# Idle transposes between TensorE's calls in the tail of a transformer block, with places and turned weights in another bank

## The chip, the cores and the metric

The kernel runs on 1 core of one Trainium2 chip. The metric is the device time in microseconds (us), the median over runs of the same program.

## The reference

One block of a Perceiver-like model in float32, over 32 sequences of 32 positions and 256 features (1024 rows, held as 8 tiles of 128 rows, four sequences in each):

```python
x = x + cross_attention(layernorm(x), ctx, ctx, mask)   # ctx: 32 x 257 x 256, 16 heads of 16
x = x + self_attention(layernorm(x))                    # causal, rotary, 16 heads
x = x + experts(layernorm(x))

# experts, in 8 groups of 128 rows, 8 experts, 32 places for each expert in each group:
raw = softmax(x @ router_w); idx1, idx2 = the two largest
p1 = cumsum(m1) - m1                      # place of a row in its expert's list
p2 = cumsum(m2) - m2 + count(m1)
combine = gate1 * onehot(idx1) * onehot(p1) + gate2 * onehot(idx2) * onehot(p2)   # where p < 32
dispatch = combine != 0
inp = einsum('GSEC,GSM->EGCM', dispatch, x)
hidden = gelu(inp @ w0) * (inp @ w1)      # 256 -> 1368
out = einsum('EGCM,GSEC->GSM', hidden @ wo, combine)
```

## The kernel before, in words

Five engines run programs of their own and meet at semaphores. The work has four stretches.

1. Preparation: weights are turned on TensorE and split in a rounded high part and a low part. A product of two such operands is three matmuls (`product3`, L213 to L217).
2. The attention pipeline (L750 to L790, to about 296 us): a loop over the 8 tiles, in which cross attention of a tile's four sequences overlaps with self attention of the tile before and the router of the one before that.
3. The tail (about 296 to 360 us): what remains of the last three tiles, `y_ - 1` = 5, `y_` = 6 and `z` = 7. Each engine has its calls in an order written out by hand: TensorE from L832, ScalarE from L1169, VectorE from L1639, GpSimd from L1855. Here cross attention's last projection is done (`project_cross`), self attention of tiles 6 and 7 (`project_self`, `turn_qk`, `scores`, `turn_self_probs`, `self_outputs`, `project_out`), the router of tiles 5 to 7 (`turn_router`, `logits`, `choose`), the places of rows (`positions` on TensorE, `place_early` and `slots_of` on VectorE), the weights of the combination (`weigh`, L1564 to L1567, 128x256 for each tile), and the dispatch (`disperse` L1619 on VectorE, `dispatch` L815 on TensorE, `keep_inputs` L1160 on ScalarE). `turn_weights_of` (L829) transposes the weights of two tiles, and `keep_weights_of` (L1166) copies them out.
4. The experts (360 to 553 us): 88 steps of 18 matmuls each, `up` and `down`, and then the combination (L925) and the store.

An engine works strictly in the order of its calls, so a wait holds everything written behind it. PSUM has eight banks, `bk[0]` to `bk[7]`. In the tail `bk[4]` belongs to tile 7, `bk[6]` to tile 6, `bk[7]` to tile 5, and the scores lie in the upper parts of banks 0 to 3. `positions(0, EARLY)` (tiles 0 to 4 in one call) writes to bank 5, the even dispatches to banks 5 and 2, the turned weights to bank 3. VectorE's `choose_early(1)` picks the second expert of tiles 0 to 4. The experts can begin when all of XT_hi and XT_lo is written (semaphore r_x_kept) and all four pairs of turned weights are copied out (ct_read).

Of the kernel before, what the change touches and what calls it, by code (L numbers as in the profile page):

```python
# [64 lines left out]
def program(nc, stack, x, ctx_in, mask, weights, xbq, xbk, xbv, xbo, router, w0, w1, wo, table, out):  # L65
# [205 lines left out]

    def positions_at(t):

        return bk[{0: 5, TT - 3: 7, TT - 2: 6, TT - 1: 4}[t]]

    def last_at(t):

# [1 line left out]

    def inputs_of(t):  # L280

        return (bk[0], bk[1]) if t % 2 else (bk[5], bk[2])

    crossed_T = bk[7][:, D:2 * D]

# [142 lines left out]
    def _(pe):  # L428
# [184 lines left out]
        def project_cross(t):  # L613
            if not exists(t, TT):
                return
            pe.wait_ge(sm["a_oT_hi"], t + 1)
            pe.wait_ge(sm["a_oT_lo"], t + 1)
            if isinstance(t, int) and t == TT - 1:
                pe.wait_ge(sm["pt1_ready"], B)
            for k in range(KH):  # L620
                last = product3(pe, front(t)[:, 0:D], OT_hi[:, k, :], OT_lo[:, k, :], WT_hi[:, 3, k, :], WT_lo[:, 3, k, :],
                                k == 0, k == KH - 1)
            last.then_inc(sm["a_wo_made"], 1)


        def turn_norm(t):
            if not exists(t, TT):
                return
            pe.wait_ge(sm["b_y"], t + 1)
            for k in range(KH):  # L630
                last = pe.transpose(front(t)[:, k * P:(k + 1) * P], y1[:, k * P:(k + 1) * P], ident)
            last.then_inc(sm["b_yT_made"], 1)

        def project_self(t, of_values):
            if not exists(t, TT):
                return
            if of_values:
                pe.wait_ge(sm["b_cos"], t + 1)
                pe.wait_ge(sm["b_sin"], t + 1)
            else:  # L640
                pe.wait_ge(sm["b_yT_hi"], t + 1)
                pe.wait_ge(sm["b_yT_lo"], t + 1)
            for n, i in enumerate((6,) if of_values else (4, 5)):
                for k in range(KH):
                    last = product3(pe, front(t)[:, n * D:n * D + D], yT_hi[:, k, :], yT_lo[:, k, :],
                                    WT_hi[:, i, k, :], WT_lo[:, i, k, :], k == 0, k == KH - 1)
            last.then_inc(sm["b_v_made" if of_values else "b_qk_made"], 1)
# [29 lines left out]
        def turn_self_probs(t):  # L677

            if not exists(t, TT):
                return  # L680
            pe.wait_ge(sm["b_pn"], t + 1)
            pe.wait_ge(sm["b_scaled"], t + 1)
            for g in range(G):
                last = pe.transpose(spare(t)[:, g, :], pr2[:, g, :, :], ident)  # L684
            last.then_inc(sm["b_pT_made"], 1)

        def after_self(t, scored):

            if not exists(t, TT):
                return  # L690
            if scored:
                pe.wait_ge(sm["b_scaled"], t + 1)
            else:
                pe.wait_ge(sm["b_pT_act"], t + 1)
                pe.wait_ge(sm["b_pT_dve"], t + 1)
# [20 lines left out]
        def project_out(t):  # L716
            if not exists(t, TT):
                return
            pe.wait_ge(sm["b_oT_hi"], t + 1)
            pe.wait_ge(sm["b_oT_lo"], t + 1)  # L720
            if isinstance(t, int) and t == TT - 3:
                pe.wait_ge(sm["a_sum"], TT)
            for k in range(KH):
                last = product3(pe, back(t)[:, 0:D], O2T_hi[:, k, :], O2T_lo[:, k, :], WT_hi[:, 7, k, :], WT_lo[:, 7, k, :],
                                k == 0, k == KH - 1)
            last.then_inc(sm["b_wo_made"], 1)
# [67 lines left out]
        def positions(t0, t1):  # L794

            n = (t1 - t0) * E
            pe.wait_ge(sm["r_chosen"], max(t0 - EARLY + 2, 1))
            if t0 == 0:
                pe.wait_ge(sm["a_lT"], TT)
            at_ = positions_at(t0)  # L800
            pe.matmul(at_[:, 0:2 * n], before, chosen[:, :, t0:t1, :], start=True, stop=True)
            pe.matmul(at_[:, 2 * n:3 * n], ones[:, :], chosen[:, 0, t0:t1, :], start=True, stop=True)              .then_inc(sm["r_pos_made"], 1)

        def dispatch(t):
# [11 lines left out]
                                     start=True, stop=True)  # L816
            last.then_inc(sm["r_x_made"], 1)

        def turn_weights_of(i):

            pe.wait_ge(sm["r_weighed"], 2 * i + 2)
            if i >= 1:
                pe.wait_ge(sm["ct_read"], i)
            else:
                pe.wait_ge(sm["b_pT_act"], TT)
                pe.wait_ge(sm["b_pT_dve"], TT)
            for q in range(4):
                t, k = 2 * i + q // 2, q % 2
                last = pe.transpose(bk[3][:, q * P:(q + 1) * P], C_all[:, t, k * P:(k + 1) * P], ident)  # L829
            last.then_inc(sm["ct_made"], 1)  # L830

        y_, z = TT - 2, TT - 1  # L832
        project_self(y_, True)
        after_self(y_ - 1, False)
        turn_probs(B - 1, (B - 1) % 4, 0)
        turn_probs(B - 1, (B - 1) % 4, 1)
        turn_qk(y_)
# [2 lines left out]
        turn_last(z)  # L840
        scores(y_)
        project_cross(z)
        project_out(y_ - 1)
        turn_norm(z)
        project_self(z, False)
        turn_self_probs(y_)
        project_self(z, True)
        turn_qk(z)
        self_outputs(y_)
        scores(z)  # L850
        turn_router(y_ - 1)
        logits(y_ - 1)
        turn_self_probs(z)
        project_out(y_)
        self_outputs(z)
        positions(0, EARLY)
        project_out(z)
        turn_router(y_)
        turn_router(z)
        logits(y_)  # L860
        dispatch(0)
        positions(y_ - 1, y_)
        dispatch(1)
        logits(z)
        dispatch(2)
        positions(y_, z)
        dispatch(3)
        dispatch(4)
        turn_weights_of(0)
        turn_weights_of(1)  # L870
        turn_weights_of(2)
        positions(z, TT)
        dispatch(y_ - 1)
        dispatch(y_)
        dispatch(z)
        turn_weights_of(3)
        pe.wait_ge(sm["r_x_kept"], TT)
        pe.wait_ge(sm["ct_read"], 4)

# [50 lines left out]
    def _(ac):  # L930
# [114 lines left out]
        def split_norm(t):  # L1045
            keep(t, "b_yT_made", yT_hi[:, :, :], halves(front(t)[:, 0:D]), "b_yT_hi")

        def keep_self_keys(t):
            keep(t, "b_qkT_made", kT[:, :, :], halves(front(t)[:, D:2 * D]), "b_kT")
# [113 lines left out]

        def keep_weights_of(i):
            ac.wait_ge(sm["ct_made"], i + 1)
            ac.activation(CT[:, 2 * i:2 * i + 2, :, :], bk[3].rearrange("p (t k n) -> p t k n", t=2, k=2), ACT.Copy)\  # L1166
              .then_inc(sm["ct_read"], 1)

        y_, z = TT - 2, TT - 1  # L1169
        keep_self_values(y_)  # L1170
        keep_probs(B - 1, (B - 1) % 4)
        keep_self_keys(y_)
        keep_last(z)
        split_cross(z)
        self_exp(y_)
        split_norm(z)
        spread_probs(y_)
        keep_self_values(z)
        keep_self_keys(z)
        self_exp(z)  # L1180
        split_self(y_)
        keep_router(y_ - 1)
        spread_probs(z)
        split_self(z)
        keep_router(y_)
        router_exp(y_ - 1)
        router_exp(y_)
        keep_router(z)
        keep_inputs(0)
        router_exp(z)  # L1190
        keep_inputs(1)
        keep_inputs(2)
        keep_inputs(3)
        keep_weights_of(0)
        keep_weights_of(1)
        keep_inputs(4)
        keep_weights_of(2)
        keep_inputs(y_ - 1)
        for n in range(3):
            split(0, n)  # L1200
        keep_inputs(y_)
        keep_inputs(z)
        keep_weights_of(3)
# [18 lines left out]
    def _(ve):  # L1222
# [425 lines left out]
        add_and_norm(z, "b", 0)  # L1648
        shift_scores(y_)
        add_and_norm(z, "b", 1)  # L1650
        split_norm(z)
        add_probs(y_)
        choose_early(1)
        scale_probs(y_)
        rotate(z)
        add_rotated(z)
        spread_probs(y_)
        add_and_norm(y_ - 1, "c", 0)
        spread_queries(z)
        scale_scores(z)  # L1660
        shift_scores(z)
        add_and_norm(y_ - 1, "c", 1)
        add_probs(z)
        scale_probs(z)
        split_self(y_)
        spread_probs(z)
        read_logits(y_ - 1)
        add_and_norm(y_, "c", 0)
        split_self(z)
        place_early()  # L1670
        weigh(0)
        add_and_norm(y_, "c", 1)
        add_and_norm(z, "c", 0)
        disperse(0)
        choose(y_ - 1)
        add_and_norm(z, "c", 1)
        weigh(1)
        weigh(2)
        disperse(1)
        weigh(3)  # L1680
        weigh(4)
        read_logits(y_)
        disperse(2)
        choose(y_)
        read_logits(z)
        disperse(3)
        slots_of(y_ - 1)
        disperse(4)
        choose(z)
        weigh(y_ - 1)  # L1690
        slots_of(y_)
        disperse(y_ - 1)
        weigh(y_)
        slots_of(z)
        disperse(y_)
        weigh(z)
# [210 lines left out]
```

## Time and profile before

| what | us |
|---|---|
| median of 3 runs | 563.48 |
| lowest, highest | 556.87, 567.03 |
| the profiled execution's own time | 566.69 |
| its span | 564.8 |
| TensorE busy, share of the span | 501.6 (89%) |
| VectorE busy | 406.2 (72%) |
| ScalarE busy | 325.1 (58%) |
| GpSimd busy | 247.3 (44%) |

The span runs from the first to the last instruction; 1.9 us of the profiled execution lie around it. The granted clock is the share of full speed that TensorE's throttle let through; its mean over this span is 0.940.

### The profile page before, as it was taken

To read this page: it belongs to the slowest core of one execution; us is meant where nothing else is said; L and a number is where in the kernel's file an instruction comes from. 1 tells how busy PE (TensorE), PEld (TensorE's weight loads), DVE (VectorE), ACT (ScalarE), POOL (GpSimd) and SP (SyncE) were. 2 spreads that over 40 slices of the span, in tenths; PEclk is the share of its full clock that TensorE was granted. 3 is DMA by queue.
4 is the path that set the end of the run, shared out by engine and by line. 5 is a ranking of instruction groups with operands and counts; after the bars stand their busy time and mean duration, and the time that the engine had idled before them with its cause. 6 is when DMAs were issued, how large, how long until landed. Compare 5 with 4: busy or idle time off the path is not lost.

```text
span 564.8 us, 18262 instructions
## 1 busy us (share of the span) xinstructions
PE 501.6 (89%) x6637; PEld 460.1 (81%) x6637; DVE 406.2 (72%) x1005; ACT 325.1 (58%) x839; POOL 247.3 (44%) x337
## 2 busy tenths in 40 slices
PE   0777999989999999999976657899999999999996
PEld 0656778878889898888865546799999999999995
DVE  6414346477666767676676788599999999999973
ACT  0325667577667757676752215666665766657650
POOL 1301153344445364444430120366667667676650
PEclk9989899999999999999996765599999999999998
DMA  7420111121111111120006200055655656465302
GB/s 217 129 94 19 38 43 40 27 55 22 42 39 35 26 33 38 21 54 2 4 2 200 102 0 1 5 196 167 188 158 189 198 174 195 146 187 188 113 1 74
DMA packets 57981, 48.91 MB, mean 87 GB/s; under 512 B 20926, under 2 KB 49600, under 8 KB 57920
## 3 DMA queue, kind: packets, MB, share of 16 engines
q1 hardware_dynamic: 57920, 48.09, 28.9%
q8 instruction: 39, 0.64, 0.5%
q14 instruction: 22, 0.18, 0.1%
HBM read 46.86 MB, written 1.08 MB: 85 GB/s over the span
## 4 chain that ended last, share of the span: by engine, by line
PE 77%; ACT 7%; DVE 5%; issue 5%; DMA 2%; SPq 2%; POOL 0%; DVEq 0%; ACTq 0%; POOLq 0%
PE bank L215 20%; PE bank L217 18%; PE bank L216 18%; PE bank L556 5%; PE bank L534 3%; PE bank L580 3%; ACT Pr L994 2%; PE bank L491 2%; PE bank L925 2%; PE bank L711 1%; ACT PTd L1087 1%; DMA bias_raw<-in_L_xattn_bv 1%; PE bank L673 1%; DMA last_prob<-Pr 1%; PE bank L684 1%
## 5 line engine op out<-in xcount | busy, mean ns | idle before, releaser
L215 PE MATMUL bank<-XT_lo,W_hi 128*128 128x256 f32 (+1 forms) x352 | 100.5, 286 | 1.3 <-ACT CT L1166 1.3
L216 PE MATMUL bank<-XT_hi,W_lo 128*128 128x256 f32 (+1 forms) x352 | 100.1, 284 | 0.0
L217 PE MATMUL bank<-XT_hi,W_hi 128*128 128x256 f32 (+1 forms) x352 | 99.8, 284 | 0.0
L1876 POOL TENSOR_TENSOR W_lo<-raw,W_hi 128x256 fp32r<-128x256 f32 (+1 forms) x88 | 88.4, 1005 | 7.0
L1799 POOL TENSOR_TENSOR Pr<-Pr,rinv 128x1028 f32<-128x1028 f32 x31 | 58.9, 1901 | 51.1 <-DVE rinv L1307 50.4
L994 ACT ACTIVATE Pr<-Sc,nmax 128x257 f32<-128x257 f32 x128 | 63.8, 502 | 23.1 <-DVE nmax L1296 21.6
L1296 DVE CUSTOM_DVE_ANT_0 Sc<-bank,mask_add 128x257 f32<-128x257 f32 x128 | 46.9, 422 | 38.8 <-PE bank L534 16.8
L1738 DVE TENSOR_TENSOR hid_lo<-hid,hid_hi 128x256 fp32r<-128x256 f32 (+1 forms) x88 | 73.1, 831 | 1.5 <-ACT hid_hi L1215 1.5
L1708 DVE TENSOR_TENSOR W_lo<-raw,W_hi 128x512 fp32r<-128x512 f32 (+1 forms) x88 | 68.8, 784 | 5.2 <-ACT W_hi L1139 1.4
L1874 POOL CAST W_hi<-raw 128x256 fp32r<-128x256 f32 (+1 forms) x88 | 39.1, 444 | 74.3 <-PE bank L217 36.9
L215 PEld LDWEIGHTS bank<-XT_lo,W_hi 128*128 128x128 f32 (+1 forms) x352 | 66.6, 189 | 1.6 <-issue 1.6
L216 PEld LDWEIGHTS bank<-XT_hi,W_lo 128*128 128x128 f32 (+1 forms) x352 | 66.4, 189 | 0.0
L217 PEld LDWEIGHTS bank<-XT_hi,W_hi 128*128 128x128 f32 (+1 forms) x352 | 66.3, 188 | 0.0
L1211 ACT ACTIVATE act<-bank 128x256 f32<-128x256 f32 (+1 forms) x88 | 33.7, 383 | 53.9 <-PE bank L217 53.3
L1139 ACT ACTIVATE W_hi<-raw 128x512 fp32r<-128x512 f32 (+1 forms) x88 | 53.6, 612 | 0.0
L215 PE MATMUL bank<-W_lo,hid_hi 128*128 128x256 f32 (+1 forms) x176 | 49.7, 282 | 0.5 <-issue 0.5
L216 PE MATMUL bank<-W_hi,hid_lo 128*128 128x256 f32 (+1 forms) x176 | 49.5, 281 | 0.0
L217 PE MATMUL bank<-W_hi,hid_hi 128*128 128x256 f32 (+1 forms) x176 | 49.5, 281 | 0.0
L1215 ACT ACTIVATE hid_hi<-hid 128x256 fp32r<-128x256 f32 (+1 forms) x88 | 36.9, 419 | 14.2 <-DVE hid L1733 12.3
L1733 DVE TENSOR_TENSOR hid<-bank,act 128x256 f32<-128x256 f32 (+1 forms) x88 | 36.4, 414 | 11.8 <-ACT act L1211 11.5
L215 PE MATMUL bank<-WT_lo,ctxT_hi 128*128 128x256 f32 x128 | 40.1, 314 | 4.7 <-ACT KT L971 4.5
L215 PE MATMUL bank<-ctxT_lo,WT_hi 128*128 128x256 f32 x128 | 39.4, 308 | 1.5 <-DVE ctxT_lo L1281 1.5
(234 smaller groups left out, 1333.4 us busy)
## 6 DMA issues: line engine op xcount, KB each, us to landing
raw<-in_L_ffn_w_kernel SPq DMA_DIRECT2D x32, 512.0 KB, 4.6
ctx_raw<-in_ctx SPq DMA_DIRECT2D x32, 256.0 KB, 2.8
raw<-in_L_ffn_wo_kernel SPq DMA_DIRECT2D x16, 512.0 KB, 5.8
raw<-in_L_ffn_w_kernel SPq DMA_DIRECT2D x16, 344.0 KB
last_prob<-Pr SPq DMA_DIRECT2D x128, 1.0 KB, 1.8
raw<-in_L_ffn_wo_kernel SPq DMA_DIRECT2D x8, 256.0 KB
x_sb<-in_x SPq DMA_DIRECT2D x4, 256.0 KB, 3.9
VL_all<-vl_rows SPq DMA_DIRECT2D x8, 128.0 KB
```

The lines of the kernel that those rows point to most:

```text
L215: pe.matmul(dst, a_hi, b_lo, start=first, stop=False)
L216: pe.matmul(dst, a_lo, b_hi, start=False, stop=False)
L217: return pe.matmul(dst, a_hi, b_hi, start=False, stop=last)
L994: ac.activation(Pr[:, r % 2, g, 0:SC], Sc[:, r % 2, g, 0:SC], ACT.Exp, bias=nmax[:, r % 2, g:g + 1], scale=-1.0, accum_out=Pr[:, r % 2, g, ...
L1139: ac.activation(W01_hi[:, (NT * half_ + n) % RW, :, :, 0:w].rearrange("p i k n -> p (i k) n"), raw01[:, :, :, t * P:t * P + w].rearrange(" ...
L1215: ac.activation(hid_hi[0:w, m % RW, :], hid[0:w, m % RH, :], ACT.Copy).then_inc(sm["hhi_done"], 1)
L1296: ve.tensor_tensor_reduce(Sc[:, r % 2, g, 0:SC], bk[g][:, 0:SC], mask_add[:, :], -0.25, 3e38, ALU.add, ALU.min, nmax[:, r % 2, g:g + 1]).t ...
L1708: ve.tensor_tensor(W01_lo[:, (NT * half_ + n) % RW, :, :, 0:w].rearrange("p i k n -> p (i k) n"), raw01[:, :, :, t * P:t * P + w].rearrang ...
L1738: ve.tensor_tensor(hid_lo[0:w, m % RW, :], hid[0:w, m % RH, :], f(hid_hi[0:w, m % RW, :]), ALU.subtract)\
L1799: po.tensor_tensor(Pr[:, r % 2, :, 0:SC], Pr[:, r % 2, :, 0:SC], rinv[:, r % 2, :].unsqueeze(2).broadcast_to([P, G, SC]), ALU.mult).then_i ...
L1874: po.tensor_copy(W2_hi[0:w, m % RW, :], raw2[0:w, t, :]).then_inc(sm["hi2"], 1)
L1876: po.tensor_tensor(W2_lo[0:w, m % RW, :], raw2[0:w, t, :], f(W2_hi[0:w, m % RW, :]), ALU.subtract)\
```

## The change

The tail alone changes.

- A new function `keep_busy(4)` issues four transposes of the identity into bank 5. They wait for nothing and nobody reads them. 34 such groups (136 transposes) stand between TensorE's calls, from behind `project_cross(z)` to behind `turn_weights_of(3)`.
- So that bank 5 is free, `positions(0, EARLY)` writes to bank 7, the even dispatches to banks 2 and 3, and the turned weights to bank 7. Waits come with it: `positions(0, EARLY)` waits for the read logits of tile 5, `positions` of tile 5 for the first weighing, `turn_weights_of(0)` for the fifth r_slot, which is an instruction of VectorE's `weigh(y_ - 1)`.
- Calls change places. TensorE: `after_self` ahead of `project_self(y_, True)`. ScalarE: `keep_probs` ahead of `keep_self_values(y_)`, `keep_self_values(z)` ahead of `spread_probs(y_)`, `split_self(y_)` ahead of `self_exp(z)`, `router_exp(y_ - 1)` ahead of `split_self(z)`, `keep_inputs(y_ - 1)` behind the first three splits of the expert weights, and others. VectorE: `choose_early(1)` ahead of `split_norm(z)`, `spread_probs(y_)` ahead of `add_rotated(z)`, `split_self(y_)` ahead of `scale_probs(z)`, `add_and_norm(y_, "c", 1)` ahead of `weigh(0)`, `choose(y_ - 1)` ahead of `disperse(0)`, `slots_of(y_ - 1)` and `weigh(4)` ahead of `read_logits(z)`, `weigh(y_ - 1)` ahead of `choose(z)`.

```diff
-        return bk[{0: 5, TT - 3: 7, TT - 2: 6, TT - 1: 4}[t]]
+        return bk[{0: 7, TT - 3: 7, TT - 2: 6, TT - 1: 4}[t]]
...
-        return (bk[0], bk[1]) if t % 2 else (bk[5], bk[2])
+        return (bk[0], bk[1]) if t % 2 else (bk[2], bk[3])
...
             if t0 == 0:
-                pe.wait_ge(sm["a_lT"], TT)
+                pe.wait_ge(sm["r_neg"], 1)
+            elif t0 == EARLY:
+                pe.wait_ge(sm["r_weighed"], 1)
...
+        def keep_busy(n):
+
+            for _ in range(n):
+                pe.transpose(bk[5][:, 0:P], ident, ident)
+
         def turn_weights_of(i):
...
             else:
-                pe.wait_ge(sm["b_pT_act"], TT)
-                pe.wait_ge(sm["b_pT_dve"], TT)
+                pe.wait_ge(sm["r_slot"], PLACE)
...
-                last = pe.transpose(bk[3][:, q * P:(q + 1) * P], C_all[:, t, k * P:(k + 1) * P], ident)
+                last = pe.transpose(bk[7][:, q * P:(q + 1) * P], C_all[:, t, k * P:(k + 1) * P], ident)
```

TensorE's calls after the change, from `project_cross(z)` on, with [n] for n groups of four idle transposes:

```
project_cross(z) [1] project_out(y_ - 1) [1] turn_norm(z) [1] project_self(z, False) [1]
turn_self_probs(y_) [1] project_self(z, True) [3] turn_qk(z) self_outputs(y_) scores(z) [1]
turn_router(y_ - 1) logits(y_ - 1) [1] turn_self_probs(z) project_out(y_) [2] self_outputs(z)
positions(0, EARLY) [1] project_out(z) [1] turn_router(y_) [3] turn_router(z) [1] logits(y_)
dispatch(0) [1] positions(y_ - 1, y_) [2] dispatch(1) [2] logits(z) [1] dispatch(2) [1]
positions(y_, z) dispatch(3) [2] dispatch(4) turn_weights_of(0) [1] turn_weights_of(1) [1]
turn_weights_of(2) positions(z, TT) dispatch(y_ - 1) [3] dispatch(y_) dispatch(z) [1]
turn_weights_of(3) [1]
```

## Rows read from the trace of the kernel before

**Rows 1.** Stretches of the span: busy us and instructions per engine, granted clock, DMA.
```profile
core 0: us, PE busy (x) PEld busy (x) DVE busy (x) ACT busy (x) POOL busy (x), PEclk, DMA share, GB/s
366.00:546.00 180.00, 180.00 (x1519) 180.00 (x1518) 168.95 (x268) 117.33 (x268) 121.57 (x168) 1.00 0.53 165
...
310.00:314.00 4.00, 3.75 (x16) 3.38 (x16) 3.22 (x10) 0.03 (x1) 0.00 (x0) 0.50 1.07 377
...
335.00:344.00 9.00, 5.14 (x22) 4.78 (x22) 8.40 (x31) 1.61 (x5) 1.71 (x3) 0.50 0.00 1
344.00:350.00 6.00, 4.99 (x21) 4.41 (x21) 5.06 (x30) 3.94 (x10) 0.00 (x0) 0.50 0.00 0
```

**Rows 2.** Timeline, TensorE: first matmuls of the experts, slow and then fast.
```profile
360.27 0.55 PE L215 MATMUL bank<-XT_lo,W_hi 128*128 128x256 f32 x1 [1.25 <-ACT CT L1166]
...
365.53 0.36 PE L215 MATMUL bank<-XT_lo,W_hi 128*128 128x256 f32 x1
```

**Rows 3.** Timeline, TensorE: transposes and small matmuls of the tail at both paces.
```profile
308.42 0.69 PE L631 MATMUL bank<-tab,y 128*128 128x128 f32 x2 [2.00 <-DVE y L1347]
...
316.13 0.64 PE L655 MATMUL bank<-tab,qk 128*128 128x128 f32 x4 [0.62 <-ACT Vm L1017]
...
343.10 1.02 PE L742 MATMUL bank<-router_sb,yTf 128*128 128x8 f32 x4 [1.88 <-ACT yTf L1017]
...
350.24 1.09 PE L829 MATMUL bank<-tab,C_all 128*128 128x128 f32 x4 [0.78 <-ACT CT L1166]
```

**Rows 4.** Chain of waits, in order of time, from the dispatches on.
```profile
346.44 2.17 PE bank L815 x8
348.61 0.87 PE bank L829 x4
...
359.38 0.65 ACT CT L1166
```

**Rows 5.** Timeline of the preparation: 16 transposes, and the next wide matmuls.
```profile
23.92 3.62 PE L446 MATMUL bank<-tab,xn 128*128 128x128 f32 x16
29.04 0.47 PE L215 MATMUL bank<-xnT_lo,WT_hi 128*128 128x512 f32 x1 [1.50 <-DVE xnT_lo L1245]
29.36 0.39 PE L216 MATMUL bank<-xnT_hi,WT_lo 128*128 128x512 f32 x1
```

**Rows 6.** Stretches: transposes and 32-column matmuls alone, then the clock.
```profile
297.00:299.00 2.00, 2.00 (x12) 1.85 (x12) 0.56 (x1) 0.60 (x1) 0.00 (x0) 0.61 0.07 1
299.00:301.00 2.00, 2.00 (x130) 1.79 (x128) 1.65 (x9) 0.39 (x1) 0.45 (x1) 0.54 0.08 5
301.00:303.00 2.00, 1.11 (x70) 0.82 (x59) 1.66 (x5) 0.75 (x3) 0.18 (x1) 1.00 0.38 48
...
314.00:316.00 2.00, 0.94 (x6) 0.77 (x6) 1.92 (x5) 1.53 (x3) 0.00 (x0) 0.88 0.25 77
```

**Rows 7.** Timeline: second choice of tiles 0 to 4, and tile 7's values.
```profile
310.78 0.14 DVE L1487 TENSOR_REDUCE gate<-rest 128x5 f32<-128x40 f32 x1
...
311.65 0.20 DVE L1494 TENSOR_TENSOR chosen<-tab,lowest 128x40 f32<-128x40 f32 x1
...
315.61 0.38 ACT L1017 ACTIVATE Vm<-bank 128x256 f32<-128x256 f32 x1 [0.45 <-PE bank L217]
```

**Rows 8.** Timeline around the turned weights and VectorE's weighing of tile 5.
```profile
348.41 1.05 PE L829 MATMUL bank<-tab,C_all 128*128 128x128 f32 x4
...
348.97 0.40 DVE L1565 TENSOR_SCALAR C_all<-tab,slot_of,gate 128x256 f32<-128x256 f32 x1
```

**Rows 9.** Waits of 310 to 360 us: who waited for what, total, times, longest.
```profile
PE bank L734 <- DVE y L1347: 8.1, 3, 3.8
...
ACT CT L1166 <- PE bank L829: 2.3, 3, 1.3
...
DVE pos L1545 <- PE bank L802: 1.5, 1, 1.5
```

More of the change, by code:

```diff
@@ L824, in turn_weights_of @@
             else:
-                pe.wait_ge(sm["b_pT_act"], TT)
-                pe.wait_ge(sm["b_pT_dve"], TT)
+                pe.wait_ge(sm["r_slot"], PLACE)
             for q in range(4):
                 t, k = 2 * i + q // 2, q % 2
-                last = pe.transpose(bk[3][:, q * P:(q + 1) * P], C_all[:, t, k * P:(k + 1) * P], ident)
+                last = pe.transpose(bk[7][:, q * P:(q + 1) * P], C_all[:, t, k * P:(k + 1) * P], ident)
             last.then_inc(sm["ct_made"], 1)
         y_, z = TT - 2, TT - 1
+        after_self(y_ - 1, False)
         project_self(y_, True)
-        after_self(y_ - 1, False)
         turn_probs(B - 1, (B - 1) % 4, 0)
@@ L842, in _ @@
         project_cross(z)
+        keep_busy(4)
         project_out(y_ - 1)
+        keep_busy(4)
         turn_norm(z)
+        keep_busy(4)
         project_self(z, False)
+        keep_busy(4)
         turn_self_probs(y_)
+        keep_busy(4)
         project_self(z, True)
+        keep_busy(4)
+        keep_busy(4)
+        keep_busy(4)
         turn_qk(z)
@@ L850, in _ @@
         scores(z)
+        keep_busy(4)
         turn_router(y_ - 1)
         logits(y_ - 1)
+        keep_busy(4)
         turn_self_probs(z)
         project_out(y_)
+        keep_busy(4)
+        keep_busy(4)
         self_outputs(z)
         positions(0, EARLY)
+        keep_busy(4)
         project_out(z)
+        keep_busy(4)
         turn_router(y_)
+        keep_busy(4)
+        keep_busy(4)
+        keep_busy(4)
         turn_router(z)
+        keep_busy(4)
         logits(y_)
         dispatch(0)
+        keep_busy(4)
         positions(y_ - 1, y_)
+        keep_busy(4)
+        keep_busy(4)
         dispatch(1)
+        keep_busy(4)
+        keep_busy(4)
         logits(z)
+        keep_busy(4)
         dispatch(2)
+        keep_busy(4)
         positions(y_, z)
         dispatch(3)
+        keep_busy(4)
+        keep_busy(4)
         dispatch(4)
         turn_weights_of(0)
+        keep_busy(4)
         turn_weights_of(1)
+        keep_busy(4)
         turn_weights_of(2)
@@ L873, in _ @@
         dispatch(y_ - 1)
+        keep_busy(4)
+        keep_busy(4)
+        keep_busy(4)
         dispatch(y_)
         dispatch(z)
+        keep_busy(4)
         turn_weights_of(3)
+        keep_busy(4)
         pe.wait_ge(sm["r_x_kept"], TT)
@@ L1165, in keep_weights_of @@
             ac.wait_ge(sm["ct_made"], i + 1)
-            ac.activation(CT[:, 2 * i:2 * i + 2, :, :], bk[3].rearrange("p (t k n) -> p t k n", t=2, k=2), ACT.Copy)\
+            ac.activation(CT[:, 2 * i:2 * i + 2, :, :], bk[7].rearrange("p (t k n) -> p t k n", t=2, k=2), ACT.Copy)\
               .then_inc(sm["ct_read"], 1)
         y_, z = TT - 2, TT - 1
+        keep_probs(B - 1, (B - 1) % 4)
         keep_self_values(y_)
-        keep_probs(B - 1, (B - 1) % 4)
         keep_self_keys(y_)
@@ L1176, in _ @@
         split_norm(z)
+        keep_self_values(z)
         spread_probs(y_)
-        keep_self_values(z)
         keep_self_keys(z)
+        split_self(y_)
         self_exp(z)
-        split_self(y_)
         keep_router(y_ - 1)
         spread_probs(z)
+        router_exp(y_ - 1)
         split_self(z)
         keep_router(y_)
-        router_exp(y_ - 1)
+        keep_router(z)
         router_exp(y_)
-        keep_router(z)
         keep_inputs(0)
+        keep_inputs(1)
         router_exp(z)
-        keep_inputs(1)
         keep_inputs(2)
@@ L1197, in _ @@
         keep_weights_of(2)
-        keep_inputs(y_ - 1)
         for n in range(3):
             split(0, n)
+        keep_inputs(y_ - 1)
         keep_inputs(y_)
@@ L1650, in _ @@
         add_and_norm(z, "b", 1)
+        choose_early(1)
         split_norm(z)
         add_probs(y_)
-        choose_early(1)
         scale_probs(y_)
         rotate(z)
+        spread_probs(y_)
         add_rotated(z)
-        spread_probs(y_)
         add_and_norm(y_ - 1, "c", 0)
@@ L1663, in _ @@
         add_probs(z)
+        split_self(y_)
         scale_probs(z)
-        split_self(y_)
         spread_probs(z)
@@ L1670, in _ @@
         place_early()
+        add_and_norm(y_, "c", 1)
         weigh(0)
-        add_and_norm(y_, "c", 1)
         add_and_norm(z, "c", 0)
+        choose(y_ - 1)
         disperse(0)
-        choose(y_ - 1)
         add_and_norm(z, "c", 1)
@@ L1680, in _ @@
         weigh(3)
-        weigh(4)
         read_logits(y_)
@@ L1684, in _ @@
         choose(y_)
+        slots_of(y_ - 1)
+        weigh(4)
         read_logits(z)
         disperse(3)
-        slots_of(y_ - 1)
         disperse(4)
+        weigh(y_ - 1)
         choose(z)
-        weigh(y_ - 1)
         slots_of(y_)
+        weigh(y_)
         disperse(y_ - 1)
-        weigh(y_)
         slots_of(z)
```

## The prediction

> **What bounds the kernel now.** I read the share of each engine in stretches of the span first. From 366 to 546 us TensorE is busy all of the time at full clock [rows 1]; those 1519 matmuls at 118 ns set the time of the experts, and nothing that the change touches makes them fewer. Next the tail, 296 to 360 us. There VectorE is the fullest engine: 8.40 of 9 us between 335 and 344 us, where TensorE has 5.14 [rows 1]. The granted clock of TensorE is 0.50, its 1.2 GHz level, from 331 us on until the experts are well under way; in all of 335 to 350 us the row says 0.50. So two things hold the tail: VectorE's own work, and in places TensorE's calls at half pace. The chain of waits shows where the second is so: 2.17 us for two dispatches and 0.87 us for a group of turned weights [rows 4]. The list of waits says the same from the other side: of TensorE's waits the longest are for VectorE (`turn_router` for y, 8.1 us in three waits), and what others wait for TensorE is short (2.3 and 1.5 us) [rows 9].
>
> **What half pace costs.** A 128x256 matmul starts every 118 ns at full clock (180 us by 1519, rows 1). From 360.27 to 365.53 us 25 of them start, one each 210 ns [rows 2]. At full clock the same 25 take 2.96 us instead of 5.26: 2.3 us, wholly on the path, because behind them TensorE doesn't pause until the end of the experts. The tail's own pieces: four transposes last 0.64 us at full clock and 1.09 at half, so with a last one of 0.27 and 0.42 us a group of four takes TensorE's time for about 0.48 and 0.87 us [rows 3, 4]; two transposes 0.69 against about 0.39; the four of `logits` 1.02 against about 0.6 (estimate, in the same ratio) [rows 3]; two dispatches 2.17 against about 1.0 for eight matmuls at 118 ns [rows 4].
>
> **The idle transposes.** 34 groups take 34 x 0.48 = 16.3 us of TensorE at full clock and 34 x 0.87 = 29.6 at half. They read and write nothing that another engine uses; only TensorE's order makes a call behind them late. To see what of it is on the path I walked the calls of the four engines in their orders, from 294 us to the experts' first matmul: a call starts when its engine is free and what it waits for is there, and lasts as its row does. The old order, at the clock that the records show, ends at 357.9 us in this walk where the trace has 360.27 [rows 2], so I use differences only.
> - Old order, full clock all through: 353.8, that is 4.1 us earlier than the old order at the shown clock. No more, though the half-paced calls on the chain hold some 6.5 us, since VectorE's 49 us of work take over: in that walk it never pauses from 328 us to the end.
> - New order with the groups, full clock all through: 353.5 (4.3 us earlier). Without the groups it is 353.3: the groups fill pauses, TensorE has 42.8 us of work in 59.
> - New order with the groups, half clock all through: 372.1, 14.2 us later. TensorE would have 73 us of work and bound the tail.
>
> **Which clock it will be.** Neither end. The trace shows rises behind stretches in which TensorE hardly paused: 310 to 314 us has 3.75 of 4 us busy at 0.50, and 314 to 316 us a mean of 0.88 [rows 1, 6]; 344 to 350 us has 4.99 of 6, with gaps, and no rise [rows 1]; the experts' start has no gap and rises after 5.3 us [rows 2]. Falls stand behind sparse stretches, such as 1.11 of 2 us from 301 to 303 us [rows 6]. At half clock the groups leave TensorE with hardly a gap, so it climbs; at full clock it is busy about 42.8 of 59 us, which is near the stretches that fell where the work is thinnest (`scores(z)` to `turn_router(y_ - 1)`, where even with a group some 2 us stay empty while VectorE shifts scores, and `turn_router(z)`, 3.4 us). So I take one or two falls, each with some us of half pace, in which the groups stand in the way: three of them ahead of `turn_qk(z)` cost 2.6 us at half pace, of which 2 are late. Walks of the new order with one to three such stretches end between 355.1 and 359.6 us, mostly 356 to 358.5; I take 356.5, 1.4 us earlier than 357.9.
>
> **Do idle transposes count as work?** The matmuls of 512 columns behind 16 transposes start 230 ns apart at 29.36 us, a pace of full clock, while the transposes took 226 ns each, half pace (the clock row reads 1.00 there all the time; the durations decide) [rows 5]. Between them TensorE had nothing. And 297 to 301 us hold only 12 transposes and 130 small instructions at a clock of 0.61 and 0.54; then it reads 1.00 [rows 6]. So transposes did go ahead of rises.
> The Trainium skill (TensorE: Matmul & The Clock Gate, Part 4: PE-mode transpose) says that a transpose doesn't count as TensorE's activity the way other matmuls do. By that the groups would be dead time; the two rises above speak against it.
>
> **The rest of the change.**
> - `positions(0, EARLY)` in bank 7 waits for logits read at 327.0 us, before it ran at 328.6: nothing. The weighing that the next `positions` waits for is 7 us old there: nothing.
> - `turn_weights_of(0)` now waits for VectorE's second step of weighing tile 5. Before, it ran at 348.41 and that step at 348.97 to 349.37 [rows 8]: 1 us late if the order stayed. But `weigh(y_ - 1)` moves ahead of `choose(z)` (2.1 us), so the wait is met before dispatch 4 ends. Nothing; 1 us if that cover goes, with `turn_weights_of(1)`, (2) and two dispatches queued behind it.
> - `choose_early(1)`, 310.78 to 311.85 us, five small dependent steps [rows 7], moves into VectorE's pause while tile 7's norm is transposed (308.4 to 309.5): 1.07 us off VectorE, but what follows waits for TensorE's projection until 313.0. Gain nothing at half clock, up to 0.5 at full.
> - `spread_probs(y_)` (1.4 us) ahead of `add_rotated(z)` makes b_rope 1.3 us later, just beside tile 7's values, 315.61 + 0.38 = 315.99 [rows 7]: 0 to 0.4 us late. On ScalarE `spread_probs(y_)` stands behind those values: 0 to 0.8 us late, with `self_outputs(y_)` behind. The last splits of the expert weights ahead of `keep_inputs(y_ - 1)` are off the last part of ScalarE's queue, 1.6 us between two dispatch copies; in the walk that is the most of the 0.3 us that the new order is worth.
> All of these are within the walks.
>
> **The sum.** 566.69 of the profiled execution, less 1.4 in the tail, less 2.3 at the experts' start (TensorE is dense in the last 10 us before it, so full clock is there): 563.0. That execution lies 3.2 above the median of 563.48, and its tail was nearly the worst that the clock can do to it (0.50 for the last 34 us). Part of the 3.2 is thus what the change takes away; I leave the new median 2.5 below 563.0: 560.5.
>
> **The rivals.**
> 1. Full clock throughout: 566.69 - 4.3 - 2.3 = 560.1, less the same 2.5: 557.6. For it: 72% mean use with the gaps spread. Against: two pauses over 2 us that no group can fill. Chance 0.25.
> 2. The groups only pay for themselves: the falls come where three groups stand, the walk ends at 359.6 (+1.7), the experts gain 2.3: 566.1, and 564 to 566 as a median. For it: 0.87 us a group at half pace. Chance 0.18.
> 3. Slower: transposes don't raise the clock, TensorE is the bound of the tail at half pace and still slow at the experts: 566.69 + 14.2 = 580.9, 578 as a median. It decides as soon as a group in a dense stretch of the tail leaves the clock at 0.50 for more than 10 us. Against it: rows 5 and 6. Chance 0.05. By the page's rule above this is the outcome.
> 4. The attention pipeline ahead of the tail and the end are untouched; nothing there moves. That the walk misses 2.4 us of the old tail leaves room for a larger gain, 5 or more beyond rival 1, below 552: chance 0.05.
> My forecast, 559 to 563: 0.47.
>
> **Range.** 553.5 to 567: from rival 1 less 4 (three runs of before spread over 10 us) to rival 2 with 1 us. A change of under 2% (11 us) is no more than runs of this kernel differ. Faster by over 2% needs 552.2 or less: 0.06; slower by over 2%: 0.05; within: 0.89.
>
> **What the profile after would show.** Right: a clock near 1.00 in most of 335 to 350 us and at the first expert matmul, these 118 ns apart; the experts' first matmul at 355 to 359 us; transposes into bank 5 lasting 0.27 us; VectorE without pauses from 330 us. Wrong: a clock of 0.50 over dense idle transposes (rival 3); `turn_weights_of(0)` waiting for VectorE; or a first matmul before 353 us, which would mean that VectorE was not the floor.

## The result and the profile after

The changed kernel takes 558.38 us (median of 12 runs, 554.31 to 561.23), the kernel before 564.77 us in 12 runs beside it (556.87 to 567.36). The ratio run against run is 0.9926, 95% interval 0.9901 to 0.9952: faster, by 0.5 to 1.0%. Twelve more runs of the changed kernel (e8), with 23 of the kernel before beside them, give 558.58 against 563.67 us, ratio 0.9897 (0.9862 to 0.9932). The profiled execution takes 558.36 us, its span is 556.4 us, 8.4 less than before.

The page of the changed kernel, engines in 40 slices of the span; the tail is in slices 22 to 26, and its clock there reads 9, 8, 8, 7, 9:

```profile
span 556.4 us, 18537 instructions
...
PE   0777999899999999999975779999999999999996
...
PEclk9999999989999999999999887999999999999998
```

Its stretches, with the columns of [rows 1]:

```profile
303.00:304.00 1.00, 0.00 (x0) 0.00 (x0) 0.97 (x2) 0.00 (x0) 0.54 (x1) 1.00 1.08 374
...
306.00:310.00 4.00, 3.94 (x21) 3.96 (x22) 2.45 (x6) 0.00 (x0) 0.00 (x0) 0.58 1.08 379
...
316.00:321.00 5.00, 2.56 (x16) 1.94 (x15) 3.91 (x8) 1.01 (x2) 1.12 (x2) 0.86 0.00 0
321.00:324.00 3.00, 3.00 (x25) 2.83 (x27) 2.13 (x6) 1.57 (x4) 0.00 (x0) 0.67 0.00 0
...
331.00:335.00 4.00, 2.14 (x12) 2.14 (x13) 3.79 (x12) 0.18 (x1) 1.87 (x4) 0.78 0.00 0
335.00:344.00 9.00, 9.00 (x62) 9.00 (x62) 7.88 (x39) 4.48 (x12) 0.00 (x0) 0.72 0.00 1
344.00:350.00 6.00, 5.32 (x46) 4.88 (x45) 4.87 (x30) 4.49 (x10) 0.00 (x0) 1.00 0.01 3
...
355.00:360.00 5.00, 5.00 (x44) 5.00 (x44) 3.52 (x6) 3.67 (x9) 4.76 (x8) 1.00 0.00 0
```

Against [rows 1]: 335 to 344 us reads 0.72 where it read 0.50, 344 to 350 us reads 1.00. The clock falls three times, each time behind a stretch in which TensorE is nearly empty and VectorE nearly full (303 to 304, 316 to 318, 329 to 333 us), and it is back at 1.00 after 3.4, 3.4 and 6.8 us of mostly dense work. The experts have 44 matmuls in the five us from 355, full pace. The timeline at their start, against [rows 2]:

```profile
354.26 0.36 PE L215 MATMUL bank<-XT_lo,W_hi 128*128 128x256 f32 x1 [0.56 <-ACT CT L1206]
```

And the idle transposes (line 824), all of them:

```profile
L824 PE MATMUL bank<-tab x136: 270/273/456, 301.2 to 353.4; 128*128 128x128 f32 x136
```

The three figures in ns are the shortest, the median and the longest: half of them last 0.27 us or less, as those of [rows 3] at full clock. No instruction waits for their result, but they stand in front of TensorE's own next call, as shown below.

To see where time went I divided each profile at two marks: the start of GpSimd's last cross-attention step (`Ot<-VL_all,last_prob`; the code before it is the same in all kernels), and the experts' first matmul. All in us, from the profiles:

| kernel | first mark | tail, first mark to first expert matmul | first expert matmul to end of span | median, ratio to before |
|---|---|---|---|---|
| before | 300.55 | 59.72 | 204.53 | 564.77 |
| changed | 297.06 | 57.20 | 202.14 | 558.38, 0.9926 |
| changed, again (e8) | 299.97 | 56.25 | 202.18 | 558.58, 0.9897 |
| e1 no groups | 301.12 | 59.92 | 204.66 | 563.58, 0.9990 |
| e2 old order, groups | 297.58 | 59.24 | 202.18 | 560.31, 0.9920 |
| e3 late groups | 296.26 | 59.50 | 202.14 | 559.64, 0.9899 |
| e12 late groups, again | 296.11 | 59.50 | 202.09 | 560.06, 0.9911 |
| e9 early groups | 295.47 | 58.00 | 201.93 | 558.41, 0.9880 |
| e4 matmuls for transposes | 295.80 | 58.01 | 202.19 | 558.80, 0.9885 |
| e6 gaps filled | 296.31 | 55.47 | 201.92 | 556.50, 0.9878 |
| e11 old order, gaps filled | 298.53 | 58.95 | 201.92 | 557.78, 0.9869 |
| e10 all filled | 295.06 | 54.17 | 200.97 | 553.06, 0.9790 |

So of the 8.4 us between the two profiles 3.5 lie ahead of the tail, in code that the change doesn't touch; the same program (changed, e8) has 2.9 us between its own two profiles there. 2.5 us (3.5 in e8) are the tail's and 2.4 the experts'. That is 4.9 to 5.9 us of the change's own, beside 6.4 and 5.1 between medians.

Within the tail the gain lies late. From the first turned weights to the experts' first matmul (the kernel before, then the changed one):

```profile
348.41:360.27 11.86, 8.18 (x33) 6.53 (x33) 8.02 (x32) 8.43 (x17) 0.04 (x1) 0.50 0.01 1
```

```profile
344.80:354.26 9.46, 7.55 (x62) 6.73 (x61) 7.58 (x33) 7.98 (x16) 0.05 (x1) 1.00 0.01 2
```

Of the tail's 2.5 us 2.4 lie here, where the clock went from 0.50 to 1.00; the 47.9 us ahead of it became 47.7 (46.8 in e8).

What lies ahead of the tail has its own clock. These are the stretches at the start of the attention pipeline in the kernel before and in e12, whose first marks are 300.55 and 296.11 us:

```profile
38.00:62.00 24.00, 19.03 (x140) 16.92 (x139) 6.88 (x23) 11.62 (x32) 2.92 (x5) 0.79 0.15 40
```

```profile
38.00:62.00 24.00, 18.31 (x233) 15.54 (x234) 10.00 (x35) 13.63 (x39) 4.71 (x6) 1.00 0.15 44
```

In the profiles of the table the clock of this stretch and the first mark go together: 0.96 to 1.00 with first marks of 295.06 to 297.06 us (changed, e3, e4, e6, e9, e10, e12), 0.79 to 0.86 with 297.58 to 301.12 us (before, e8, e1, e2, e11). The two profiles of the changed kernel, with the same code, read 1.00 and 0.86. Whole runs say the same: of the 15 of the kernel before beside e9 to e12, the five with a mean clock of 0.948 or more took 561.2 to 563.5 us, the ten with less 564.5 to 569.7. What makes the clock fall there in one execution and not in another stays open.

### The profile page after: what moved, and what is told of

Read it like the earlier page. It is cut to its first block, busy times and chain, and to the rows that moved or that the text cites. A ratio compares the mean times of both kernels' runs of the same rounds, so it can differ in the third digit from the quotient of the medians.

```text
span 556.4 us, 18537 instructions
## 1 busy us (share of the span) xinstructions
PE 502.3 (90%) x6773; PEld 463.1 (83%) x6773; DVE 404.8 (73%) x1005; ACT 324.9 (58%) x839; POOL 250.5 (45%) x337
## 4 chain that ended last, share of the span: by engine, by line
PE 78%; ACT 7%; issue 5%; DVE 4%; DMA 2%; SPq 2%; POOL 0%; DVEq 0%; ACTq 0%; POOLq 0%
PE bank L215 20%; PE bank L216 18%; PE bank L217 18%; PE bank L556 5%; PE bank L534 3%; PE bank L580 3%; ACT Pr L1034 2%; PE bank L491 2%; PE bank L824 2%; PE bank L965 2%; PE bank L711 1%; DMA bias_raw<-in_L_xattn_bv 1%; PE bank L673 1%; DMA last_prob<-Pr 1%; ACT PTd L1127 1%
## 5 line engine op out<-in xcount | busy, mean ns | idle before, releaser
L215 PE MATMUL bank<-XT_lo,W_hi 128*128 128x256 f32 (+1 forms) x352 | 99.3, 282 | 0.6 <-ACT CT L1206 0.6
L1916 POOL TENSOR_TENSOR W_lo<-raw,W_hi 128x256 fp32r<-128x256 f32 (+1 forms) x88 | 90.6, 1030 | 7.0
L1778 DVE TENSOR_TENSOR hid_lo<-hid,hid_hi 128x256 fp32r<-128x256 f32 (+1 forms) x88 | 74.9, 851 | 1.5 <-ACT hid_hi L1255 1.5
L1748 DVE TENSOR_TENSOR W_lo<-raw,W_hi 128x512 fp32r<-128x512 f32 (+1 forms) x88 | 66.5, 758 | 4.8 <-ACT W_hi L1179 1.1
L215 PEld LDWEIGHTS bank<-XT_lo,W_hi 128*128 128x128 f32 (+1 forms) x352 | 65.4, 186 | 0.8 <-issue 0.8
L216 PEld LDWEIGHTS bank<-XT_hi,W_lo 128*128 128x128 f32 (+1 forms) x352 | 65.2, 185 | 0.0
L1355 DVE COPY PT<-bank 128x512 f32<-128x512 f32 x32 | 22.1, 691 | 25.5 <-PE bank L556 25.3
```

Source lines behind the costliest of these rows:

```text
L215: pe.matmul(dst, a_hi, b_lo, start=first, stop=False)
L216: pe.matmul(dst, a_lo, b_hi, start=False, stop=False)
L1748: ve.tensor_tensor(W01_lo[:, (NT * half_ + n) % RW, :, :, 0:w].rearrange("p i k n -> p (i k) n"), raw01[:, :, :, t * P:t * P + w].rearrang ...
L1778: ve.tensor_tensor(hid_lo[0:w, m % RW, :], hid[0:w, m % RH, :], f(hid_hi[0:w, m % RW, :]), ALU.subtract)\
L1916: po.tensor_tensor(W2_lo[0:w, m % RW, :], raw2[0:w, t, :], f(W2_hi[0:w, m % RW, :]), ALU.subtract)\
```

## The experiments

**Is it the groups or the order?** e1 takes all 34 groups out, the rest as changed; this line each time:

```diff
-        keep_busy(4)
```

> The changed kernel without its 34 groups; banks, waits and orders as changed. My theory (the groups buy the clock and the clock buys the time): nearly all of the gain goes. The clock reads about 0.50 over most of the tail and at the experts' first matmuls, which start 0.21 us apart, and the ratio to the kernel before is 0.997 to 1.005. Rival (the new order of calls is the gain): the ratio stays at 0.992 to 0.994 at that same low clock.

Measured: 563.58 against 564.33 us, ratio 0.9990 (0.9962 to 1.0018). The tail is 59.92 us, the stretches of e1 read:

```profile
301.12:331.00 29.88, 19.92 (x255) 16.21 (x255) 21.16 (x52) 7.22 (x17) 3.40 (x6) 0.60 0.43 142
331.00:361.04 30.04, 18.46 (x78) 15.91 (x79) 24.21 (x105) 13.74 (x30) 2.82 (x6) 0.58 0.00 1
361.04:366.00 4.96, 4.96 (x23) 4.96 (x24) 1.51 (x3) 2.35 (x4) 4.64 (x8) 0.50 0.00 0
```

Half clock in most of the tail and at the experts' start, and no gain, as expected. At this clock the new order, with the new banks and waits, is worth nothing that shows.

**The old order with the groups.** e2 has the old sequences of all three engines, with the new banks and waits and the groups.

```diff
+        project_self(y_, True)
         after_self(y_ - 1, False)
-        project_self(y_, True)
...
-        choose_early(1)
         split_norm(z)
         add_probs(y_)
+        choose_early(1)
...
```

> Old order of calls on TensorE, ScalarE and VectorE, with the new banks and the 34 groups in their places between TensorE's calls. My theory: 0.990 to 0.995, about the whole gain, since the walks of both orders at full clock end 0.3 us apart. Rival (the order is the gain): 0.998 or more, though the clock is high.

Measured: 560.31 against 564.33 us, ratio 0.9920 (0.9882 to 0.9959), as I expected by the ratio. But the tail of its profile is 59.24 us, 2 to 3 longer than the changed kernel's, though its clock in the tail is as high (0.88 from mark to mark, as in the changed kernel). That is against the walks, which gave the order 0.3 us, though the half-paced stretches don't stand at the same calls in the two. e11 takes it up.

**Which groups?** e3 keeps the 9 behind `dispatch(4)`, e9 the 25 ahead of it.

Each takes out the same line as e1: e3 its 25 places from `project_cross(z)` to `dispatch(4)`, e9 its 9 places behind that.

> The changed kernel with only the 9 groups that stand behind dispatch(4); the 25 ahead of it are taken out. My theory: the tail up to dispatch(4) goes at half clock as before, then the clock rises at some point in the last 8 us ahead of the experts or not at all; if it rises, the experts' 2.3 us come back and the ratio is 0.995 to 0.998, if not it is 1.000. Rival (only the experts' start matters): 0.992, the full gain.

> The changed kernel with only the 25 groups ahead of dispatch(4) and none of the 9 behind. With e3 it splits the gain by place. My theory (each stretch of half clock taken away pays for itself where it stands): the tail up to dispatch(4) is as short as with the change; behind it the clock may fall again, then the experts' first matmuls start 0.21 us apart and 2.3 us are lost. Ratio 0.992 to 0.996. Rival (the end of the tail and the experts' start are all that counts, as the 4.7 us of e3 suggest): 0.997 or more.

e3: 559.64 against 564.33 us, 0.9899 (0.9867 to 0.9930). e9: 558.41 against 565.87 us, 0.9880 (0.9823 to 0.9937). Both ratios lie below what was expected (0.995 to 0.998 and 0.992 to 0.996). Stretches of e3, then of e9:

```profile
331.00:348.00 17.00, 11.48 (x50) 10.72 (x51) 15.27 (x73) 5.76 (x14) 2.77 (x5) 0.50 0.00 0
348.00:355.76 7.76, 6.14 (x50) 5.53 (x49) 5.52 (x20) 7.36 (x15) 0.04 (x1) 0.99 0.01 2
355.76:360.76 5.00, 5.00 (x42) 5.00 (x43) 2.78 (x5) 3.68 (x8) 4.68 (x8) 1.00 0.00 0
```

```profile
344.00:353.47 9.47, 4.74 (x35) 3.74 (x33) 7.60 (x33) 7.97 (x16) 0.05 (x1) 1.00 0.00 0
353.47:358.47 5.00, 5.00 (x29) 5.00 (x30) 1.62 (x3) 2.70 (x6) 4.68 (x8) 0.66 0.01 3
```

The profiles are as the theory has them. e3 keeps half clock until 348 us; then the clock comes up with the nine groups and the experts start at full pace, 42 matmuls in 5 us. Its tail is as long as the old one (59.50 against 59.72 us), but not in its parts: from the first turned weights on it takes 10.32 us where the kernel before takes 11.86, and ahead of them, at half clock nearly all the way, it is 1.3 us longer. e9 shortens the tail by 1.7 us, but the 9.47 us without late groups are half empty, the clock falls, and the experts start with 29 matmuls in 5 us: their last matmul comes 190.14 us after the first, against 188.66 in the changed kernel and 191.04 before. So the two sets work where they stand. In e9's profile the 1.5 us lost there come back at the very end, and the table's 201.93 us hides them: the clock happened to stay at 1.00 in the combination, whose 32 matmuls take 7.17 us instead of the 8.86 of the changed kernel. The medians don't show what the late groups add to the early ones: 558.41 us for e9, 558.38 and 558.58 for all 34. Nor are the medians what the profiles add up to: e3's marks explain 2.6 us, its median 4.7. So I ran it again (e12).

> The kernel of e3 once more, on another chip, since its 4.7 us were 2 us more than its profile explains (tail as long as before, experts 2.4 us shorter). If that was spread between runs: ratio 0.993 to 0.997. If it holds: 0.988 to 0.992 again, and something ahead of the tail or in it gains that one profile didn't show.

Measured: 560.06 against 565.87 us, 0.9911 (0.9881 to 0.9941). It holds, and its profile again has the old tail (59.50), 2.4 us less in the experts, and a first mark at 296.11 us, 4.4 earlier than before's. So it wasn't spread between a few runs, and what the two profiles gain beyond the experts lies ahead of the tail, where the code is the same and their clock is at 1.00 (above). Whether the late groups have a part in that is not shown: two profiles can't say whether it is more than the luck that moved the changed kernel's mark from 297.06 to 299.97.

**Do transposes count as activity?** e5 puts 100 of them in a row between the tail's last wait and the experts, in the kernel before, where the clock is 0.50.

```diff
         pe.wait_ge(sm["r_x_kept"], TT)
         pe.wait_ge(sm["ct_read"], 4)
+        for _ in range(100):
+            pe.transpose(bk[5][:, 0:P], ident, ident)
```

> The kernel before, with 100 idle transposes in one row between the last wait of the tail and the experts' first matmul, where its clock is 0.50. If transposes raise the clock: the first 16 to 32 start 0.21 us apart, the rest 0.12, the row lasts about 14 us, and the experts begin at full clock. If they don't: all 100 start 0.21 us apart, 21 us, the experts begin slow and their clock rises some 5 us in.

The row lasts 13.04 us and the kernel takes 573.26 us (one run). Timeline and stretches of e5:

```profile
358.13 13.04 PE L880 MATMUL bank<-tab 128*128 128x128 f32 x100 [1.14 <-ACT CT L1168]
370.92 0.36 PE L215 MATMUL bank<-XT_lo,W_hi 128*128 128x256 f32 x1
```

```profile
358.13:362.00 3.87, 3.87 (x19) 3.87 (x20) 0.00 (x0) 1.15 (x1) 0.00 (x0) 0.50 0.00 0
362.00:370.90 8.90, 8.90 (x83) 8.90 (x83) 0.00 (x0) 0.00 (x0) 1.47 (x4) 0.99 0.01 2
```

TensorE ran nothing but transposes in these 13 us: 0.20 us each for 3.9 us at 0.50 (1.2 GHz), then 0.107 us each at full clock (2.4 GHz). They count. The Trainium skill (TensorE: Matmul & The Clock Gate, Part 4: PE-mode transpose) has it that the full clock doesn't engage for transposes, beside figures for bf16; for these float32 transposes the measurement decides against it.

e4 asks the same in place: each idle transpose becomes an idle matmul with twice the columns.

```diff
-                pe.transpose(bk[5][:, 0:P], ident, ident)
+                pe.matmul(bk[5][:, 0:D], WT_hi[:, 3, 0, 0:P], WT_hi[:, 3, 0, :], start=True, stop=True)
```

> Each idle transpose is replaced by an idle matmul of 128x256 in float32r into the same bank: nearly the same time of TensorE (118 against 120 ns at full clock, 210 at half for both), but twice the columns. If transposes count as activity like matmuls, the time and the clock are the same as with the change (ratio 0.990 to 0.995, mean clock of the tail within 0.04 of 0.88). If they count for less, the clock falls less often and the ratio is lower by 0.002 or more.

558.80 against 564.33 us, 0.9885 (0.9845 to 0.9924); tail 58.01 us, its clock 0.88 as in the changed kernel. The ratio is 0.004 and 0.001 below those of the changed kernel (0.9926 and 0.9897); the intervals overlap, so the 0.002 of the expectation can't be told by it, and the clock of the tail shows no difference.

**What do the three falls cost?** e6 puts more into the empty stretches.

```diff
         project_out(y_ - 1)
-        keep_busy(4)
+        keep_busy(12)
         turn_norm(z)
-        keep_busy(4)
+        keep_busy(8)
...
         scores(z)
-        keep_busy(4)
+        keep_busy(18)
...
         turn_router(y_)
-        keep_busy(4)
-        keep_busy(4)
-        keep_busy(4)
+        keep_busy(36)
```

> The changed kernel with 44 more idle transposes in its three empty stretches: 8 more ahead of turn_norm(z), 4 more behind it, 14 more ahead of turn_router(y_ - 1), 24 instead of 12 more ahead of turn_router(z) in all 36. If the three falls of the clock (at 305.9, 319.2 and 333.3 us of the profile after) come from those stretches, the clock stays at 1.00 there and the tail is 1.5 to 3 us shorter than with the change: ratio 0.986 to 0.990. Rival (VectorE's work is the floor and the half-paced calls are hidden behind it): the clock stays up and the ratio is that of the change, 0.991 to 0.994.

The edit adds 8 + 4 + 14 + 24 = 50 idle transposes; the 44 of the expectation is a slip. Measured: 556.50 against 563.67 us, 0.9878 (0.9837 to 0.9919), beside 0.9897 of the changed kernel on the same chip (e8). The intervals overlap, so the medians don't settle it; the profile is clearer. From its first mark to 325 us its clock reads 1.00 throughout, one fall is left (340 to 344 us, 0.57), and the tail is 55.47 us, 0.8 and 1.7 less than the two profiles of the changed kernel.

```profile
296.31:325.00 28.69, 24.42 (x424) 21.18 (x414) 23.19 (x63) 7.23 (x17) 3.42 (x6) 1.00 0.45 149
325.00:351.78 26.78, 22.06 (x175) 20.65 (x174) 22.44 (x97) 13.41 (x30) 2.83 (x6) 0.94 0.00 1
340.00:344.00 4.00, 4.00 (x23) 3.70 (x22) 3.35 (x21) 1.92 (x4) 0.00 (x0) 0.57 0.01 4
```

> The changed kernel again, on the chip of the three runs beside it: 0.990 to 0.995.

Measured: 558.58 against 563.67 us, 0.9897 (0.9862 to 0.9932).

**Is TensorE's time free?** e7 doubles every group (`keep_busy(8)`).

> Each of the 34 groups has eight transposes instead of four, 16 us more of TensorE's time at full clock. TensorE's work in the tail is then 59 of 59 us, so it bounds the tail though its clock is 1.00 all through: 5 to 9 us longer than with the change, ratio 1.002 to 1.009. If it were no longer, TensorE's time in the tail would be free.

562.83 us, 4.3 above the changed kernel beside it and a little less than the 5 to 9 expected; ratio to before 0.9969 (0.9936 to 1.0002). Its mean clock is as high as e6's (both a median of 0.988 over their runs, 0.977 in the changed kernel), and nearly the whole gain is gone. So 16 us more of idle work on TensorE cost 4.3 us: the room for it is limited. Where the time is lost no profile shows.

**What is the order worth at full clock?** e11 is e2 with the larger groups of e6.

> The old orders of calls on all engines with the groups of e6, so that the clock is at full speed in nearly all of the tail: what is the order worth then? By the walks of the prediction 0.3 us: tail from Ot to the experts' first matmul 55.5 to 56.5 us against 55.5 of e6, ratio 0.986 to 0.989. Rival (the new order pays once TensorE is fast, as e2 hints): tail of 57 to 58.5 us, ratio 0.990 to 0.994.

557.78 against 565.87 us, 0.9869 (0.9825 to 0.9914), and a tail of 58.95 us against e6's 55.47. By the tail the rival holds, by the ratio the theory does: it is no higher than e6's 0.9878, and the medians lie 1.3 us apart in two batches of runs. The profile has to be read with care, for its execution is the slowest of e11's six (561.31 us) with the lowest mean clock (0.979, the others 0.988 to 0.994). Most of the 3.5 us goes with its clock:

```profile
298.53:308.61 10.08, 8.39 (x167) 7.93 (x159) 6.33 (x17) 1.68 (x4) 1.22 (x2) 0.66 0.80 256
```

From the first mark to `turn_norm(z)` it is 10.08 us here, at a mean clock of 0.66, and 7.74 in e6 at 1.00. That is 2.3 of the 3.5 us. That the old order brings this fall on is not shown; e2, with the same order, takes 7.54 us to `turn_norm(z)`. Half of the 2.3 us is a price of idle work when the clock has fallen all the same: the 12 transposes ahead of `turn_norm(z)` ran at half clock, and the norm waited behind them. TensorE and VectorE in e11's timeline:

```profile
306.10 2.68 PE L824 MATMUL bank<-tab 128*128 128x128 f32 x12
...
306.98 0.41 DVE L1385 TENSOR_SCALAR y<-x_sb,ln_mvb,ln_rb 128x256 f32<-128x256 f32 x1
...
308.61 0.38 PE L631 MATMUL bank<-tab,y 128*128 128x128 f32 x2
```

y is there at 307.39 and is turned at 308.61: 1.2 us late. From `turn_norm(z)` to the experts it is 48.87 us in e11 and 47.73 in e6, with a clock of 0.97 and 0.96. This 1.1 us is what the profiles leave for the order at a high clock. 0.5 of it lies between `turn_norm(z)` and `turn_router(y_ - 1)` (12.87 and 12.37 us), where `choose_early(1)` stands: in e11 it runs from 310.67 to 311.75, between the sums and `scale_probs`, and TensorE waits 0.3 us for the result; in e6 it runs in the pause before yT_lo, from 303.91 to 305.03.

**The best version.** e10 is e6 with the other idle places of the kernel filled too: 36 transposes into bank 6 while the attention pipeline fills, 20 ahead of the combination.

```diff
         turn_ctx(0, 0, 16)
+        fill(12)
         keys(0, 0)
+        fill(6)
         values(0, 0)
...
                 energies(b, u)
+                if early_ and u == 0:
+                    fill(7)
...
                     keys(b + 1, (u + 1) % 4)
+                    if early_:
+                        fill(11)
...
+        keep_busy(20)
         pe.wait_ge(sm["y_read_dve"], E + 1)
```

> The kernel of e6, with 36 more idle transposes in the gaps at the start of the attention pipeline (12 behind the first turn_ctx, 6 behind keys(0), 7 behind energies(0), 11 behind keys(1)) and 20 ahead of the combination at the very end. Theory (half clock costs wherever TensorE is on the path): the fall at about 40 us and the one ahead of the combination go, 1 to 3 us and 1 us less than e6, ratio 0.980 to 0.986, and the best version so far. Rival (there the other engines hold the pace, or the row only delays the first real calls): as e6, 0.986 to 0.990.

553.06 against 565.87 us, ratio 0.9790 (0.9748 to 0.9832), and a spread of only 3.1 us over 6 runs. Its stretches:

```profile
295.06:325.00 29.94, 25.70 (x433) 22.56 (x424) 24.54 (x65) 7.62 (x18) 3.40 (x6) 1.00 0.43 143
325.00:349.23 24.23, 19.15 (x161) 17.78 (x160) 21.07 (x94) 13.14 (x29) 2.87 (x6) 1.00 0.00 1
...
537.00:550.20 13.20, 10.05 (x58) 8.90 (x58) 4.72 (x11) 1.17 (x2) 0.00 (x0) 1.00 0.24 81
```

1.00 in all of the tail, which takes 54.17 us, and at the end, where the combination's 32 matmuls take 7.07 us instead of 8.61 in e6, and the end of the span comes 0.95 us sooner. e9's 7.17 us without any filler there show that the clock sometimes stays up by itself, so one profile each doesn't prove what the 20 transposes are worth. Nor does the first mark: 295.06 us here, 295.47 to 296.26 in the three profiles of e9, e3 and e12, whose clock was at 1.00 from 38 to 62 us without fillers. All six runs lie below every run of the changed kernel and of the kernel before (554.01 at most, 554.31 at least). More transposes later in the pipeline were not tried.

## Why the prediction held, and where it was off

- The mechanism was right: the groups buy the clock (e1 without them 0.9990), the clock gives TensorE's calls back, and the rule that spoke against it (rival 3) fell to e5.
- The term for the experts' start, 2.3 us, measured 2.4: the last expert matmul comes 191.04 us after the first before, 188.66 after.
- The term for the tail, 1.4 us, was too small: 2.5 and 3.5 us in two profiles. I had "one or two falls"; there are three, at about the places named, with 3.4, 3.4 and 6.8 us of half pace (e8 has a fourth around its first mark, 15 us in all). So the falls were not fewer than assumed; what they cost was. 2.4 us of the gain lie behind the first turned weights, where no fall stood.
- The walks gave the order 0.3 us. At half clock none of it shows (e1). At high clock it is 1.1 us between e11 and e6 from `turn_norm(z)` on, and 2 to 3 us between the tails of e2 and of the changed kernel, whose falls stand elsewhere; the medians don't tell it from nothing. So 0.3 looks too small, and by how much stays open. "Up to 0.5 at full" for `choose_early(1)` agrees with the 0.5 us of its stretch.
- VectorE as the floor of the tail is right in kind and was put too high: in e10, at 1.00 throughout, VectorE is busy 21.07 of the last 24.23 us, but the walk gave 4.3 us as the most that the clock can return, and e10's tail has 5.55 less than before.
- "Three of them ahead of `turn_qk(z)` cost 2.6 us" didn't happen: the clock was up at 310 us in both profiles. But the price is real elsewhere: eight idle transposes take 1.95 us in the timeline of the changed kernel at 337 us, and 1.2 us were lost behind twelve of them in e11.
- The two new waits cost nothing: no row of the waits after has `turn_weights_of` or `positions` waiting for VectorE's weighing for more than a few tenths.
- "0.50 for the last 34 us" of the old tail is a slip in the reading: 5.3 of the 34 us are the experts' [rows 2], and ahead of 331 us the tail's clock goes up and down.
- Of the signs named, the transposes of 0.27 us and the full pace of the experts came as said. The clock of 335 to 350 us was only half right (0.72 to 344 us, then 1.00), the experts' first matmul came at 354.26 us, ahead of the 355 to 359 named, with a first mark 3.5 us early, and VectorE did pause (4.87 us busy of 6 from 344 us).
- That the number came within 2.1 us is in part luck. The sum gave 563.0 us for an execution like the profiled one; the new one took 558.36, of which 3.5 lie ahead of the tail, where nothing was forecast to move, and 1.1 in the tail. The 2.5 us taken off for the median stood in for them by chance: profile and median of the changed kernel are equal. The median of 558.38 lies below the 559 to 563 of the forecast, close to rival 1's 557.6, whose condition (full clock throughout) didn't hold. The spread ahead of the tail, up to 2.9 us within one program, is as large as the terms that were argued about.

## What to carry to other kernels

Where TensorE waits for others and its granted clock is at half, find the stretches at half pace and ask which of its calls there are on the path; idle work ahead of a dense stage can pay even if the tail itself is no shorter (e3: 2.4 us at the experts). Fill the empty stretches themselves rather than every gap: a filler costs nearly double where the clock has fallen already (twelve transposes 2.68 us in e11, 1.47 in e6), and doubled groups gave back most of the gain (e7). Before a difference between two profiles is put down to the code, compare their clock stretch by stretch, ahead of the changed part too: 2.3 of the 3.5 us between e11 and e6 and some 4 us ahead of the tail (before against e12) went with the clock of that execution.

## What was not expected of the hardware

- In a row of 100 float32 transposes and nothing else the clock goes from 0.50 to 1.00 after 3.9 us (e5); groups of idle ones give the same clock in the tail, 0.88, as matmuls of twice the columns (e4).
- A transpose of 128x128 in a dense row takes 0.107 us at full clock (83 in 8.90 us), less than the 0.12 that groups of four suggested.
- The same program can differ by 2.9 us ahead of the tail between two executions (297.06 and 299.97 us), and the clock from 38 to 62 us differs with it (1.00 and 0.86). The kernels with late groups alone gain 2 to 3 us more by their medians than their tail and experts explain, on two chips; whether the groups have a part in it is open.
